# Expert weights handed over with the contracted axis in front, halves made from SBUF, a bank for each expert step, and the addition one expert later

## The reference

```python
g = jnp.einsum('ecd,eid->eci', buf, W1)      # 16 experts, up to 128 slots, D = 256, I = 176
u = jnp.einsum('ecd,eid->eci', buf, W3)
h = jax.nn.silu(g) * u
out = jnp.einsum('eci,edi->ecd', h, W2)
y = (out[e, posc] * w).reshape(T, K, D).sum(axis=1)          # K = 2 experts per token
gs = jax.nn.silu(xt @ Ws1.T); us = xt @ Ws3.T                # the shared expert
return y + (gs * us) @ Ws2.T
```

## Time and profile before

| | |
|---|---|
| runs | 449.58, 450.5, 446.66 us; median 449.58 |
| profiled execution | 448.65 us, its span 446.9 us |
| busy share of the span | PE 86%, PEld (weight loads) 66%, DVE 67%, ACT 58%, POOL 19% |
| PE's share in the chain that ended last | 76% |

### The profile page before, as it was taken

The page is one execution under the profiler, slowest core; times in us unless marked ns, Lnnn a source line. Parts: engine busy times, 40 slices in busy tenths (PEclk is TensorE's granted clock), DMA queues, the critical chain, the costliest instruction groups (busy, mean ns, idle before and its releaser), DMA issues.

```text
span 446.9 us, 14782 instructions
## 1 busy us (share of the span) xinstructions
PE 385.0 (86%) x6066; PEld 294.3 (66%) x6066; DVE 300.4 (67%) x646; ACT 257.9 (58%) x421; POOL 83.1 (19%) x89
## 2 busy tenths in 40 slices
PE   0298796999999999998999999876639899999993
PEld 0256365767768767766768778654528788888882
DVE  2972682676676686685686676674696767777772
ACT  3335473677678677676677666645114365666660
POOL 7521930222222123124023100000020100000000
PEclk9999696999999999999999999989856699999999
DMA  8349997176176185294172176000010234334401
GB/s 243 61 74 217 216 186 152 49 136 167 49 139 165 51 163 138 62 169 120 53 137 72 31 123 153 7 4 1 1 48 1 49 94 101 97 97 109 123 12 41
DMA packets 40734, 43.74 MB, mean 98 GB/s; under 512 B 3942, under 2 KB 40278, under 8 KB 40678
## 3 DMA queue, kind: packets, MB, share of 16 engines
q1 hardware_dynamic: 39878, 41.89, 42.1%
q0 software_dynamic: 800, 1.04, 1.4%
HBM read 23.24 MB, written 0.46 MB: 53 GB/s over the span
## 4 chain that ended last, share of the span: by engine, by line
PE 76%; DVE 10%; issue 5%; ACT 3%; POOL 2%; DMA 2%; SPq 1%; POOLq 0%; DVEq 0%; ACTq 0%
PE PS L907 33%; PE PS L982 9%; PE PS L971 9%; PE PS L949 9%; PE PS L1171 3%; PE PS L1154 3%; DMA c_in<-ctx 2%; PE PS L1055 2%; PE PS L959 2%; PE PS L1048 1%; SPq L290 1%; PE PS L1191 1%; DVE mx L676 1%; DVE am L603 1%; PE PS L1161 1%
## 5 line engine op out<-in xcount | busy, mean ns | idle before, releaser
L676 DVE TENSOR_REDUCE mx<-PS 112x1 f32<-112x500 f32 (+1 forms) x128 | 114.4, 934 | 68.3 <-PE PS L949 68.3
L460 ACT ACTIVATE PT_all<-PS 128x1344 f32<-128x1344 f32 x64 | 82.6, 1290 | 14.1 <-PE PS L971 14.1
L907 PE MATMUL PS<-wkvT,cT 128*125 128x256 f16 x576 | 72.9, 278 | 3.5 <-issue 3.5
L907 PE MATMUL PS<-cT,wkvT 128*128 128x500 f16 x288 | 72.4, 393 | 4.0 <-POOL cT L397 3.9
L907 PEld LDWEIGHTS PS<-wkvT,cT 128*125 128x125 f16 x576 | 65.0, 139 | 8.8 <-issue 4.1
L397 POOL TENSOR_TENSOR cT<-c_in,cT 128x1000 f16<-128x1000 f32 x21 | 43.7, 2084 | 99.5 <-ACT cT L440 99.5
L971 PE MATMUL PS<-QC,arena 98*128 98x112 f16 x768 | 49.2, 214 | 7.5 <-ACT QC L480 4.9
L907 PEld LDWEIGHTS PS<-cT,wkvT 128*128 128x128 f16 x288 | 28.5, 101 | 38.2 <-issue 6.1
L949 PE MATMUL PS<-arena,QC 96*112 96x500 f16 x192 | 53.3, 386 | 0.0
L447 ACT ACTIVATE KN<-PS,bk_c 128x500 f16<-128x500 f32 x48 | 32.5, 677 | 34.2 <-PE PS L907 34.2
L971 PEld LDWEIGHTS PS<-QC,arena 98*128 98x128 f16 x768 | 41.7, 99 | 13.7 <-ACT QC L480 5.5
(11 more groups left out here) (203 smaller groups left out, 459.0 us busy)
## 6 DMA issues: line engine op xcount, KB each, us to landing
arena<-KN SPq DMA_DIRECT2D x144, 125.0 KB, 3.9
c_in<-ctx SPq DMA_DIRECT2D x24, 500.0 KB, 5.8
c_in<-L_ffn_W SPq DMA_DIRECT2D x48, 176.0 KB
q<-PT_all POOLq DMA_DIRECT2D x6, 112.0 KB, 5.1
c_in<-L_ffn_Ws SPq DMA_DIRECT2D x3, 176.0 KB
PT_all<-L_xattn_wkv SPq DMA_DIRECT2D x1, 512.0 KB, 4.8
x_in<-x SPq DMA_DIRECT2D x1, 448.0 KB, 4.1
y<-xn SPq DMA_DIRECT2D x1, 448.0 KB, 3.2
```

Source lines behind the costliest of these rows:

```text
L460: act.activation(PT_all[:, u % 4, :].rearrange("p (c k) -> p c k", c=CH), PS[:, 3:6, 0:4 * TP], ACT.Exp, scale=SCORE).then_inc(s["exp_done ...
L676: dve.tensor_reduce(mx[:, u % 2, k:k + 1], PS[0:TP, k:1 + k * (CH - 1), 0:CW], AX.XY, ALU.max).then_inc(s["red_done"], 1)
L907: ins = mm(out_, w(a, h), x_(b, h), start=first and k == 0, stop=last and k == len(todo) - 1)
```

## The change

The host hands over W1 with W3 and Ws1 with Ws3 as one array `W13`, and W2 with Ws2 as `W2`, with the contracted axis in front; index 0 is the shared expert, e + 1 is expert e. No weight is transposed on the chip. High and low halves are made from the fp32 weights in SBUF. There are six homes for weights (two in `c_in`, four in `cT`, free after attention's last projections), two DMAs per expert. Gates, turned hidden values, results, tokens, turned slots and slot sums have a PSUM bank each. `y low` and `y high` of e-1 move to the head of step e on VectorE and ScalarE, `select` runs two experts ahead, w13_lo becomes VectorE's last work of a step, and there are three `selT` buffers. The loop is written out, so the credits and the two memsets go.

```diff
+NW = 6
+        WIN = 2 * NH * I + 2 * D
+        w_homes = [c_flat[:, k * WIN:(k + 1) * WIN] for k in range(2)] + [cT_flat[:, k * WIN:(k + 1) * WIN] for k in range(NW - 2)]
-        selT = [over_keys(CAP, T) for i in range(2)]
+        selT = [over_keys(CAP, T) for i in range(3)]
...
-        g_bank = (2, 3, 6, 2)
-        h_bank = (3, 2)
+        g_bank = (2, 4, 5, 7)
+        h_bank = (3, 6)
+        place_bank = 2
+        gather_bank, gu_bank, turn_bank, y_bank, slot_bank, sum_bank = 2, 3, 4, 5, 6, 7
...
+            def load_weights(j):
+                if j == 0:
+                    need(sp, "tl_done", CH * (B - 1))
+                if j == 2:
+                    need(sp, "k_ready", 6 * B)
+                    need(sp, "v_ready", 6 * B)
+                need(sp, "w13l_done", j - NW + 1)
+                need(sp, "w2l_done", j - NW + 1)
+                sp.dma_start(w13_in[j % NW], W13[j]).then_inc(w_in[j % NW], 16)
+                sp.dma_start(w2_in[j % NW], W2[j]).then_inc(w_in[j % NW], 16)
...
-            for name in credited:
-                gp.sem_inc(s[name], 1)
-            gp.memset(selT[1], 0.0).then_inc(s["added_init"], 1)
-            gp.memset(y16[:], 0.0).then_inc(s["added_init"], 1)
...
+            def w2_hi(j):
+                act.wait_ge(w_in[j % NW], 32 * (j // NW + 1))
+                need(act, "y_ready", j - 2)
+                act.activation(w2T[j % 2][:, 0], w2_in[j % NW], ACT.Copy, scale=FS).then_inc(s["w2h_done"], 1)
+            def w13_hi(j):
+                need(act, "gu_ready", j - 2)
+                act.activation(w13T[j % 2][:, 0], w13_in[j % NW], ACT.Copy, scale=FS).then_inc(s["w13h_done"], 1)
...
+            def expert(e):                                   # ScalarE
+                if e > 0:
+                    result_hi(e - 1)
+                if e + 1 < E:
+                    if e > 0:
+                        w2_hi(e + 2)
+                need(act, "gu_ready", e + 1)
+                need(act, "h_done", e)
+                act.activation(th_e, PS[:, gu_bank, 0:I], ACT.Tanh, scale=0.5 / FS).then_inc(s["tanh_done"], 1)
+                if e + 1 < E:
+                    w13_hi(e + 2)
+                    tokens_hi(e + 1)
+                need(act, "ht_ready", e + 1)
+                act.activation(heT[:, 0, :], PS[0:IH, turn_bank, 0:2 * CAP], ACT.Copy).then_inc(s["hh_done"], 1)
+                if e + 1 < E:
+                    slots_turned(e + 1)
...
             def slot_weights(e):
-                after(dve, "st_ready", e + 1)
-                after(dve, "st_done", e + 1)
-                after(dve, "h_done", e)
+                need(dve, "st_ready", e + 1)
+                need(dve, "h_done", e)
...
+            def gates_and_ups(e):
+                need(pe, "w13l_done", e + 2)
+                need(pe, "xg_done", e + 1)
+                need(pe, "h_done", e)
+                split3(PS[:, gu_bank, 0:2 * I], ...)
+            def results(e):
+                need(pe, "hl_done", e + 1)
+                need(pe, "w2l_done", e + 2)
+                need(pe, "yl_done", e)
+                split3(PS[:, y_bank, 0:D], ...)
+            for e in range(E):                               # TensorE
+                gates_and_ups(e)
+                if e + 1 < E:
+                    gather(e + 1)
+                    turn_slots(e + 1)
+                turn_hidden(e)
+                if e > 0:
+                    add(e - 1)
+                results(e)
```

More of the change, by code:

```diff
@@ L531, in _ @@
             act.activation(sp_row[:], PS[0:TP, 1, D:2 * D], ACT.Copy, scale=tg[0:TP, 0:1]).then_inc(s["act_weights"], 1)
-            weights_hi(1, 1)
+            w2_hi(0)
+            w13_hi(0)
             for k in range(2):
@@ L586, in _ @@
             act.wait_ge(s["shared_y"], 2)
             tokens_hi(0)
-            slots_turned(0, 0)
-            with act.Fori(0, E // 2 - 1) as it:
-                for q in range(2):
-                    expert(it * 2 + q, q, True)
-            expert(E - 2, 0, True)
-            expert(E - 1, 1, False)
+            slots_turned(0)
+            w2_hi(2)
+            for e in range(E):
+                expert(e)
+            result_hi(E - 1)
         @block.vector
@@ L842, in _, with select @@
             d.settle()
-            post_steps = d.n
-            def select(e, q, first=False):
-                if not first:
-                    after(dve, "st_ready", e - 1)
-                dve.tensor_tensor(sel[q], slots[:].unsqueeze(1).to_broadcast([TP, TT, CAP]),
-                                  place[:, bass.ds(e * TT, TT)].unsqueeze(2).to_broadcast([TP, TT, CAP]),
+            def select(e):
+                need(dve, "st_ready", e - 1)
+                dve.tensor_tensor(sel[e % 2], slots[:].unsqueeze(1).to_broadcast([TP, TT, CAP]),
+                                  place[:, e * TT:(e + 1) * TT].unsqueeze(2).to_broadcast([TP, TT, CAP]),
@@ L877, in expert @@
                     slot_weights(e + 1)
-                after(dve, "yh_done", e + 1)
-                dve.scalar_tensor_tensor(y16[:, 1, :], PS[:, 2, 0:D], 1.0 / FS, y16[:, 0, :], ALU.mult, ALU.subtract).then_inc(s["yl_done"], 1)
-                assert own.n == 1
+                need(dve, "hh_done", e + 1)
+                dve.tensor_tensor(heT[:, 1, :], PS[0:IH, turn_bank, 0:2 * CAP], heT[:, 0, :], ALU.subtract).then_inc(s["hl_done"], 1)
+                if e + 1 < E:
+                    w13_lo(e + 2)
@@ L882, in _ @@
             dve.wait_ge(s["dve_post"], 5)
-            select(0, 0, first=True)
-            w2_lo(2, 0)
-            w13_lo(2, 0)
+            select(0)
+            select(1)
+            w2_lo(1)
+            w13_lo(1)
             slot_weights(0)
-            with dve.Fori(0, E // 2 - 1) as it:
-                for q in range(2):
-                    expert(it * 2 + q, q, True)
-            expert(E - 2, 0, True)
-            expert(E - 1, 1, False)
-            after(dve, "added", E + 1)
+            for e in range(E):
+                expert(e)
@@ L893, in _ @@
+            result_lo(E - 1)
+            need(dve, "added", E)
             for t in range(TT):
```

256 lines of the change are left out of this document (97 added, 159 removed).

## The result

The kernel after the change takes **433.96 us** (median of 4 runs, 431.94 to 439.81) against 448.66 us (4 runs, 446.66 to 450.5) of the kernel before, timed beside it: a ratio of **0.9643, 95% interval 0.9582 to 0.9705**. It is faster by 3.0 to 4.2%. Ratios and their intervals leave out executions in the chip's slower state (here the one of 439.81 us), the medians do not. The forecast was 436.0 us, range 432.0 to 442.5.

The account below looks back on a forecast made before the run. The prediction took the loop to be bound by TensorE's own order; gains of 9.9 (loop), 0.85 (first gates), 1.7 (credits) and 0.5 (memsets) summed to 13.0 us, giving 436.0 us, range 432.0 to 442.5.

Parts of the forecast that it names:

- The steady loop: Expert loop: each of 15 steps falls from 5.11 to 4.45 us, a gain of 9.9 us.
- The rings: Expert loop: two dependency chains close over one step, through w13_lo to gates and through VectorE's order, both 4.47 us.
- ring two: Expert loop: VectorE's order from hg through heT low, y low and select to the next hg, 4.47 us.
- The bound from TensorE's order: Expert loop: heT low, results, then next gates bound the step from below at 4.34 us.
- The credits: Kernel start: without GpSimd's 22 semaphore increments its constants and rstd come earlier, 1.7 us gained.
- The memsets: Second normalisation, before the loop: without GpSimd's two memsets VectorE's normalise runs faster, 0.5 us gained, bounds 0 and 0.6.
- Gates of expert 0: Loop entry: gates no longer wait for slot_w and start once the tokens are in SBUF, 0.85 us gained.
- the first rival: The forecast itself: step 4.34 to 4.65 us, at least half the front gains kept, 433.5 to 439.5 us; chance 0.66.
- The chain longer than its legs: Expert loop: other queued ScalarE and VectorE work lengthens the step to 4.65 to 5.0 us, 439.5 to 445; chance 0.19.
- TensorE as the bound: Expert loop: TensorE's own work still sets the step, near 3.9 us, time 427.6 us; chance 0.03.
- the removed work was hidden: Expert loop: no steady gain, step 5.0 us or more, time within 1% of 449 us; chance 0.05.
- The clock: Expert loop: with holes TensorE loses its granted clock, step about 7.0 us, time 450 to 474 us; chance 0.04.

Follow-up runs that it names:

- e3: The changed kernel with twelve dead fp32 transposes per step put back on TensorE; 448.06 us, ratio 0.9972 to the kernel before.
- e4: The changed kernel, still without transposes, with the old waits on slot_w and selT's eviction and the old order put back; 442.48 us, ratio 0.9869 to the kernel before.
- variants: The changed kernel with one or two edits each (increments, transposes, waits, memsets, VectorE order or pipelining); times from 428.22 to 448.06 us.
- second execution of before: The kernel before run once more without any edit; 446.89 us in one run.
- e2: The kernel before with only GpSimd's 22 credits moved behind its small loads; 447.62 us, ratio 0.9948 to the kernel before.
- second execution of after: The changed kernel profiled once more without any edit; the runs of this repeat have a median of 433.44 us.
- the second timing: The changed kernel timed again without any edit, 4 runs; 433.44 us, ratio 0.9678 to the kernel before.
- e6: The changed kernel with gates and ups of expert e+1 issued right behind the turn of e's hidden values; 428.22 us, ratio 0.9598 to the kernel before.
- e7a: The changed kernel with VectorE's select moved from ahead of hg to behind w13_lo; 435.55 us in one run.
- e7b: The changed kernel with w13_lo and w2_lo swapped in VectorE's order, w13_lo directly behind hn; 435.91 us in one run.

## Why the prediction was right

**The steady loop: right.** 15 × (5.11 − 4.45) = 9.9 us was said; 76.6 − 66.5 = 10.1 us is measured. That the chain of the last expert "is what remains once TensorE is relieved" held: legs read at 435 to 440 us of the old trace gave the new step to 0.02 us. The legs as they stand sum to 4.47, and most of the 0.04 between this and 4.43 is the leg from turn to heT high, 0.52 in the last expert and 0.46 in after's loop (371.90 to 372.36). The rings were named rightly. That they tie was close, but not exact: ring two is 4.39. The bound from TensorE's order, 4.34, measured 4.29.

**What bound the old loop: not wholly TensorE's own order.** The prediction read only matmul rows and found no idle entry. The weight loads and slot_w of the same step of the kernel before show a wait:

```profile
393.55 0.45 PEld L1048 LDWEIGHTS PS<-ident,c_in 128*88 128x88 f32 x4
...
393.90 0.23 DVE L858 TENSOR_SCALAR slot_w<-PS 128x1 f32<-128x1 f32 x1 [0.26 <-issue]
...
394.24 0.72 PEld L907 LDWEIGHTS PS<-arena 128*128 128x128 f16 x6 [0.24 <-issue]
...
430.01 1.06 PE L907 MATMUL PS<-arena 128*128 128x352 f16 x6
```

The loads for gates come 0.24 us late, 0.11 behind the end of slot_w, for which gates wait. The four transposes of w2 ahead of gates took 0.61 us start to start in the earlier trace rows but 0.44 in e3 (385.03 to 385.47), so some 0.17 of the 0.61 is this wait. No transposes of w2 stand ahead of the gates of the last expert, yet these come 5.09 us behind the gates before them (430.01 to 435.10), released by slot_w. So in the kernel before the transposes of w2 ran beside a wait that ended no earlier than they did, and by these rows taking them alone away would have brought nothing (not run). That fits e4, where all twelve together bring only 0.31 to 0.36 us of the 1.22. The 3.89 us for TensorE's own work came out right all the same: the 0.17 us of wait stand both in the step of 5.11 and in the 1.22 taken off it.

The old steps of 5.16 and 5.06 us in turn, against 5.08 behind the loop, show one thing more: the hardware loop may have cost about 0.03 us a step, 0.4 us in all. The prediction took 0 for unrolling. No run takes this apart from the rest of the 10.1 us.

**The credits: right.** 1.7 said; 11.48 − 9.76 = 1.72 us, the new chain at the start being these rows, to set against the earlier trace rows (start us, us, what):

```profile
0.80 1.35 POOL arena L327
...
8.68 1.05 POOL rstd L360
9.73 0.03 issue
9.76 1.39 DVE xn L634 x4
```

**The memsets: right,** 0.5 said, 0.6 measured.

**Gates of expert 0: the step worked, its size was wrong.** The prediction took 0.85 us. Gates are now released by the tokens, as it said, 0.14 us behind their eviction:

```profile
351.18 0.60 ACT L556 ACTIVATE arena<-PS 128x512 f16<-128x512 f32 x1 [6.32 <-PE PS L1125]
...
351.92 1.05 PE L904 MATMUL PS<-arena 128*128 128x352 f16 x6 [0.53 <-ACT arena L556]
```

But from the logits to tanh(0) are 20.5 to 20.8 us in three executions of the kernels before and 20.2 to 20.5 in after and those variants that keep its waits: about 0.3 us (e4, with the old waits, has 21.2). From the start of the first gather to gates it was 3.30 us and is 2.76 us in after (from 349.16), so 0.54 of the 0.85 is there; the gather itself starts 0.3 us later against the logits. The term counted a wait for slot_w as if nothing ahead of it would move. In the traces of this pair the 0.3 us are one wait of VectorE for ScalarE in the router, 0.32 us at 338.87 in after and none in before. The other executions pair otherwise. In the second execution of before and in e2 the gather waits for select and starts 1.28 us behind the operation that places the tokens (`place`). In the second execution of after and in the variants it stands behind the shared expert's last 12 matmuls, which take 2.79 us at a granted clock of 0.50 (2.33 and 2.20 us in the two named before), and starts 1.5 to 1.8 us behind `place`. The first executions of both kernels have 2.79 us there and 1.53 to 1.54. So the gather's start hangs on TensorE's clock in this stretch too. Whether the missing transposes lower it, where the prediction took 0 for the shared expert, no run separates.

**Sum.** 10.1 + 1.7 + 0.6 + 0.3 = 12.7 us against 13.0 said, the loop 0.2 over and the gates 0.55 under. The medians show 14.7 us, and the ratio 3.0 to 4.2% (13.2 to 18.8 us); the second timing gives 2.5 to 3.9%. 12.7 us are 2.8%: inside the second and just under the first. The 4 us beyond it in the first pair of traces are the spread of attention, as the second executions and e3 show. A small real gain could be in it: e3's interval leaves room for some 0.7 us, and the end of the program took 1.2 to 1.3 us longer in two of the three executions with the old loop (the clock of 0.72) and in none of after or its variants except e6, whose end is longer at a clock of 1.00. That stays open. So the steps were right, but how close the time came, 434.0 for 436.0, is in part chance. One slip of the prediction: its own terms put the lower end of the first rival at 434.4 (449 − 15 × 0.77 − 3.05), not at 433.5.

**The rivals.** The chain longer than its legs (step 4.65 to 5.0) is out at 4.433. tanh starts 1.09 us after gates in expert 0 (351.92 to 353.01), just inside the 1.1 that the prediction set as its limit; in the second execution of after it is 1.65 us there, where the six matmuls of gates took 1.62 in place of 1.05 us, without harm to the steps behind it. That hg would wait for select is out by e7a: without select ahead of it the step stays. TensorE as the bound (3.9) was out for this kernel, and e6 shows what it would have been: 3.90. That the removed work was hidden is out by e3 for the twelve transposes together; those of w2 alone are another matter, as said above. The clock is out: 1.00 in the loop with two holes in every step. The Trainium skill's case (TensorE: Matmul & The Clock Gate, section on psum-queue depth-cycling) didn't come up here, though this kernel cycles through six banks with a hole of 0.25 to 0.30 us twice in 4.43.

**Wrong: the sign by which the holes would show.** The prediction wanted TensorE's busy share in the loop at 85 to 93%. The row reads 58.97 of 60.30 us, 98%. The ends of matmuls are modelled, and a group that waits for a late weight load is drawn across the hole: `PE L904 ... x12` at 417.56 spans 1.86 us and covers both results and gates. The weight-load row has the holes, from 88 to 77%. The Trainium skill (Perfetto Trace Analysis, section on the most-contended engine) says that the busy share of matmuls is not a good measure and names the weight-load share, beside a count of the arithmetic done, instead. The trace agrees, though here the matmul row reads too full, where the reason that the Trainium skill gives is that such rows look too short.

**A little off: the tie of the rings.** Priced alike, nothing should have moved when one alone was cut. In e7a nothing did; in e7b the step lost 0.04 us, which is how far apart they are.

## What to carry to other kernels

When an engine is full, removing its work gives only as much as the next ring allows: look for a place in the old trace where the work stands without cover (here the last expert), add its legs start to start, and close the ring over one step through every engine's order. Read the weight loads too before an engine is called full. Two bounds can need lifting together: transposes alone 0.31 us, waits and order alone 0, both 0.68. Then look whether the order, not the work, is the new bound; here one expert more of pipelining (e6) gave another 0.53 us a step.

## What the runs showed of the hardware that wasn't expected

A low half made from SBUF takes as long as one made from PSUM, w13_lo in after and in before (count, ns min/median/max, first and last start):

```profile
L742 DVE SCALAR_TENSOR_TENSOR arena<-cT,arena x11: 876/878/879, 355.4 to 417.4; 128x704 f16<-128x704 f32 x11
```

```profile
L744 DVE SCALAR_TENSOR_TENSOR arena<-PS,arena x17: 876/877/878, 326.5 to 433.6; 128x704 f16<-128x704 f32 x17
```

w2_lo: 678 and 677 ns. Either form also reads the high half from SBUF. ScalarE is slower from SBUF: w13_hi 782 against 752 ns, w2_hi 617 against 583 ns. The Trainium skill (VectorE: DVE Perf Modes, section on the TRN2 errata) gives VectorE 62 fixed cycles less from SBUF than from PSUM and ScalarE 52 more. For this VectorE operation, with one input from SBUF in both forms, the rows show no difference, and the measurement decides; for ScalarE they agree in sign and roughly in size.

The span of attention, identical code, varies by up to 7 us from one execution to the next (299.8 to 307.0), more than all terms of this change outside the loop together. A single pair of spans can't size such a term; the stretch in which it stands can, since the steps of after's loop repeat to 0.02 us.
